# An adaptive-norm mixture-of-experts layer: reloading the higher expert's rows in four stages

## The reference

```python
# condition: base projection plus a low-rank adapter chosen per sequence
c = x @ W.T + b + 2 * ((x @ A[slot]) @ B[slot])          # x: 32 sequences x 32 tokens x 512
# router: 16 experts in 4 groups; the two best groups are kept, then the two best experts
scores = softmax(c @ router_w + router_b) + router_bias
idx = top-2 of the kept scores;  gate = the scores at idx  (zero elsewhere)
for e in 16 experts:                                      # scan
    h = silu(c @ w1[e] + b1[e]) * (c @ w2[e] + b2[e])     # 512 -> 128
    y = y + gate[:, e] * (h @ w3[e] + b3[e])              # 128 -> 512
z = silu(c @ sw1 + sb1) * (c @ sw2 + sb2) @ sw3 + sb3     # shared expert, 512 -> 256 -> 512
out = x + y + z
```

## Time and profile before

| | |
|---|---|
| median of 3 runs | 160.32 us (159.95 to 160.36) |
| the profiled execution | 158.57 us |
| its span, first to last instruction | 156.7 us |
| mean granted TensorE clock | 0.994 |
| busy: PE, DVE, ACT, POOL | 92%, 57%, 42%, 34% |
| HBM read, written | 31.98 MB, 8.91 MB |

### The profile page before, as it was taken

The page is one execution under the profiler, slowest core; times in us unless marked ns, Lnnn a source line. Parts: engine busy times, 40 slices in busy tenths (PEclk is TensorE's granted clock), DMA queues, the critical chain, the costliest instruction groups (busy, mean ns, idle before and its releaser), DMA issues.

```text
span 156.7 us, 3059 instructions
## 1 busy us (share of the span) xinstructions
PE 144.9 (92%) x954; PEld 113.9 (73%) x955; DVE 89.3 (57%) x225; ACT 65.6 (42%) x111; POOL 53.1 (34%) x69
## 2 busy tenths in 40 slices
PE   3999999999989999999999999999897989599990
PEld 3877666877757788888988878887685867188750
DVE  2781484288777679978517434452222240479992
ACT  3542341641722351155876575494554463300000
POOL 7740220000000020536425676667274736340000
PEclk9999999999999999999999999999999999999997
DMA  4989998999985799916541648868685399836993
GB/s 163 355 262 309 409 328 311 345 400 413 418 287 228 228 372 384 391 38 189 145 129 76 193 125 268 287 201 242 226 217 188 105 311 409 319 138 196 375 353 151
DMA packets 16671, 41.09 MB, mean 262 GB/s; under 512 B 2352, under 2 KB 2352, under 8 KB 16528
## 3 DMA queue, kind: packets, MB, share of 16 engines
q1 hardware_dynamic: 11392, 23.33, 42.1%
q0 software_dynamic: 3776, 12.59, 24.9%
q10 hardware_dynamic: 1488, 4.98, 8.3%
HBM read 31.98 MB, written 8.91 MB: 261 GB/s over the span
## 4 chain that ended last, share of the span: by engine, by line
PE 74%; DVE 12%; ACT 4%; issue 4%; another core or an unknown queue 2%; POOL 1%; DVEq 1%; ACTq 1%; POOLq 0%
PE bank L986 27%; PE bank L1166 18%; PE bank L1177 9%; PE bank L1151 5%; DVE x_sb L937 3%; DVE x_sb L950 3%; PE bank L1049 3%; PE bank L1081 2%; PE bank L1029 2%; DVE x_sb L945 2%; PE bank L1039 1%; PE bank L1006 1%; PE bank L1060 1%; PE bank L1141 1%
## 5 line engine op out<-in xcount | busy, mean ns | idle before, releaser
L1166 PE MATMUL bank<-xgT_sb,w_now 128*128 128x128 f32 x288 | 35.2, 275 | 0.0
L1166 PEld LDWEIGHTS bank<-xgT_sb,w_now 128*128 128x128 f32 x288 | 33.6, 192 | 0.6 <-issue 0.5
L875 DVE SCALAR_TENSOR_TENSOR hT_sb<-bank,b_sb,glT_sb 128x128 f32<-128x128 f32 x18 | 6.3, 350 | 38.3 <-ACT glT_sb L614 17.7
L467 POOL DMA_INDIRECT y_rows<-y_ring,slot_row x18 | 19.4, 1079 | 20.5 <-DVE y_ring L883 18.2
L461 POOL DMA_INDIRECT xg_sb<-xt_rows,slot_tok x22 | 21.2, 965 | 13.2 <-issue 5.2
L1177 PE MATMUL bank<-w_sb,hT_sb 128*128 x36 | 18.9, 607 | 4.1 <-DVE hT_sb L875 4.1
L609 ACT COPY w_now<-w_sb 128x1024 f32 x18 | 18.7, 1046 | 3.5 <-issue 2.1
L603 ACT COPY xgT_sb<-bank 128x512 f32<-128x512 f32 x18 | 10.5, 584 | 16.7 <-PE bank L1151 10.6
L1151 PEld LDWEIGHTS bank<-ident,xg_sb 128*128 128x128 f32 x72 | 8.9, 141 | 8.0 <-issue 7.9
L986 PE MATMUL bank<-condW_h,xT_h 128*128 128x512 f32 x32 | 14.4, 449 | 0.0
L986 PE MATMUL bank<-xtT_h,sw_h 128*128 128x512 f32 x32 | 13.2, 412 | 0.0
(11 more groups left out here) (166 smaller groups left out, 240.7 us busy)
## 6 DMA issues: line engine op xcount, KB each, us to landing
w_sb<-in_w SPq DMA_DIRECT2D x8, 1024.0 KB, 10.3
w_sb<-in_w ACTq DMA_DIRECT2D x2, 2048.0 KB, 16.5
xt_rows<-xt_ring SPq DMA_DIRECT2D x8, 256.0 KB, 5.5
x_sb<-in_x SPq DMA_DIRECT2D x8, 256.0 KB
low_sb<-y_rows SPq DMA_DIRECT2D x4, 512.0 KB
high_sb<-y_rows SPq DMA_DIRECT2D x4, 512.0 KB, 5.9
out<-x_sb SPq DMA_DIRECT2D x8, 256.0 KB, 3.2
xT_raw<-in_xT SPq DMA_DIRECT2D x3, 512.0 KB, 8.5
```

Source lines behind the costliest of these rows:

```text
L467: pool.indirect_dma_start(y_rows, bass.IndirectOffsetOnAxis(ap=slot_row[:, b:b + 1], axis=0), y_place(b), None).then_inc(y_scattered[b % Y ...
L875: dve.scalar_tensor_tensor(out=hT_sb[:, s % 2, :], in0=up_bank(s)[:, 0:P], scalar=b12_sb[:, bass.ds(2 * e + 1, 1)], in1=glT_sb[:, s % 2, : ...
L1166: mm = pe.matmul(half[:, 0:P], w12_now[:, s % 2, (2 * k + m) * INTER:(2 * k + m + 1) * INTER], xgT_sb[:, s % 2, k, :], start=(k == 0), sto ...
```

## The change

The one wait for all blocks before the high reload becomes four, one for each pair of tiles. For stages 0 to 2, VectorE works out from `rank` the slot by which every used expert has passed the tokens of that pair of tiles and the earlier ones; stage 3 needs all blocks. With these inputs the stages need 12, 14, 16 and 18 blocks; the low reload needs 10 as before. SP reads 4 low counts and 16 stage counts (20 in place of 8) before the low reload. The high rows are reloaded to a place behind the low rows in `low_sb`, with an address from a register, and `high_sb` is gone. VectorE's tail takes the tiles one by one: low, high, shared; TensorE's wait for banks 5 and 6 is now for the first finished tile.

```diff
@@ names and tiles
-STORED_AT, LOW_STORED_AT = BPAD + 4, BPAD + 4 + Y_RING
+STORED_AT = BPAD + 4
+LOW_STORED_AT = STORED_AT + TILES // 2 * Y_RING
+STAGES = TILES // 2 + 1
-        low_sb = at(0, "low_sb", [P, UPPER_W12 + TILES * DIM])
-        high_sb = at(16, "high_sb", [P, TILES, DIM])
-        diag = at(48, "diag", [P, len(LOW_ON_PE), P])
+        low_sb = at(0, "low_sb", [P, UPPER_W12 + 2 * TILES * DIM])
+        diag = at(104, "diag", [P, len(LOW_ON_PE), P])
-        rows_stored = sem("rows_stored")
+        rows_stored = [sem(f"rows_stored{n}") for n in range(TILES // 2)]
@@ SP
             low_counts = stored(sp, LOW_STORED_AT, LOW_BLOCKS)
-            counts = stored(sp, STORED_AT, FULL)
+            counts = [stored(sp, STORED_AT + n * Y_RING, LOW_BLOCKS) for n in range(TILES // 2)]
@@
-            for s in range(Y_RING):
-                sp.wait_ge(y_scattered[s], counts[s])
-                sp.sem_inc(rows_stored, 1)
-            sp.wait_ge(rows_stored, Y_RING)
             for n in range(TILES // 2):
-                sp.dma_start(high_sb[:, 2 * n:2 * n + 2], by_tile[1][:, 2 * n:2 * n + 2]).then_inc(high_in[n], 16)
+                for s in range(Y_RING):
+                    sp.wait_ge(y_scattered[s], counts[n][s])
+                    sp.sem_inc(rows_stored[n], 1)
+                sp.wait_ge(rows_stored[n], Y_RING)
+                sp.dma_start(low_tiles(first, TILES + 2 * n, 2).rearrange("p (i d) -> p i d", i=2),
+                             by_tile[1][:, 2 * n:2 * n + 2]).then_inc(high_in[n], 16)
@@ VectorE, before the loop
-            then(dve.tensor_scalar(nused_f[:], ends[0:1, E - 1:E], 1.0 / P, None, ALU.mult))
-            then(dve.tensor_scalar(low_base[:], padded[0:1, :], 0, None, ALU.is_gt))
-            then(dve.tensor_tensor(low_base[:], low_base[:], base[0:1, :], ALU.mult))
-            then(dve.tensor_reduce(low_slots[:], low_base[:], AX.X, ALU.max))
+            LAST, LOW = TILES // 2 - 1, TILES // 2
+            then(dve.tensor_scalar(used[:], padded[0:1, :], 0, None, ALU.is_gt))
+            then(dve.tensor_tensor(low_base[:], used[:], base[0:1, :], ALU.mult))
+            then(dve.tensor_tensor(need_e[:], rank[0:1, 2:TILES:2, :], used[:].unsqueeze(1).to_broadcast([1, LAST, E]), ALU.mult))
+            then(dve.tensor_reduce(need[:, LOW:], low_base[:], AX.X, ALU.max))
+            then(dve.tensor_reduce(need[:, 0:LAST], need_e[:], AX.X, ALU.max))
+            then(dve.tensor_copy(need[:, LAST:LOW], ends[0:1, E - 1:E]))
+            then(dve.tensor_scalar(need_i[:], need[:], float(P - 1), None, ALU.add))
+            then(dve.tensor_scalar(need_i[:], need_i[:], P.bit_length() - 1, None, ALU.arith_shift_right))
@@
-            then(dve.tensor_scalar(low_f[:], low_slots[:], 1.0 / P, None, ALU.mult))
-            then(dve.tensor_scalar(stored_i[:, 0], slots_back[:], nused_f[:, 0:1], None, ALU.add))
-            then(dve.tensor_scalar(stored_i[:, 1], slots_back[:], low_f[:, 0:1], None, ALU.add))
+            then(dve.tensor_copy(need[:], need_i[:]))
+            then(dve.tensor_tensor(stored_i[:], need[:].unsqueeze(2).to_broadcast([1, STAGES, Y_RING]),
+                                   slots_back[:].unsqueeze(1).to_broadcast([1, STAGES, Y_RING]), ALU.add))
@@ VectorE's tail: the order of the passes
-            low 0, shared 0, low 1, low 2, shared 1, low 3, shared 2, low 4, shared 3, high 0, high 1,
-            shared 4, high 2, high 3, shared 5, high 4, high 5, high 6, shared 6, high 7, shared 7
+            low 0, high 0, shared 0, low 1, high 1, shared 1, low 2, high 2, shared 2, low 3, high 3, shared 3,
+            low 4, high 4, shared 4, high 5, shared 5, high 6, shared 6, high 7, shared 7
-            (shared adds count acc_shared and wait for it, the last pass of a tile counts acc_done)
+            (every low and high pass waits for itself, every shared add counts acc_done and waits for nothing)
@@ TensorE
                 if shared_bank(i) in (bank[5], bank[6]):
-                    pe.wait_ge(acc_shared, 1)
+                    pe.wait_ge(acc_done, 1)
```

More of the change, by code:

```diff
@@ L189, in program @@
         ngroups = sb("ngroups", [1, 1], I32)
-        nused_f = sb("nused_f", [1, 1])
-        low_f = sb("low_f", [1, 1])
+        used = sb("used", [1, E])
         slots_back = sb("slots_back", [1, Y_RING])
-        stored_i = sb("stored_i", [1, 2, Y_RING], I32)
-        eid = sb("eid", [1, BPAD + 4 + 2 * Y_RING], I32)
+        stored_i = sb("stored_i", [1, STAGES, Y_RING], I32)
+        need_e = sb("need_e", [1, TILES // 2 - 1, E])
+        need = sb("need", [1, STAGES])
+        need_i = sb("need_i", [1, STAGES], I32)
+        eid = sb("eid", [1, BPAD + 4 + STAGES * Y_RING], I32)
         low_base = sb("low_base", [1, E])
-        low_slots = sb("low_slots", [1, 1])
         upper_empty = sb("upper_empty", [1, 1])
-        rows_stored = sem("rows_stored")
+        rows_stored = [sem(f"rows_stored{n}") for n in range(TILES // 2)]
         rank = lgs
@@ L247, in program @@
         y_scattered = [sem(f"y_scattered{s}") for s in range(Y_RING)]
-        shared_done, acc_shared = sem("shared_done"), sem("acc_shared")
+        shared_done = sem("shared_done")
         diag_ready = sem("diag_ready")
@@ L857, in _ @@
             then(dve.tensor_scalar(slots_back[:], cols[0:1, 0:Y_RING], -1.0, float(Y_RING - 1), ALU.mult, ALU.add))
-            then(dve.tensor_scalar(nused_f[:], ends[0:1, E - 1:E], 1.0 / P, None, ALU.mult))
-            then(dve.tensor_scalar(low_base[:], padded[0:1, :], 0, None, ALU.is_gt))
-            then(dve.tensor_tensor(low_base[:], low_base[:], base[0:1, :], ALU.mult))
-            then(dve.tensor_reduce(low_slots[:], low_base[:], AX.X, ALU.max))
+            LAST, LOW = TILES // 2 - 1, TILES // 2
[7 more added lines that the diff above has]
+            then(dve.tensor_scalar(need_i[:], need_i[:], P.bit_length() - 1, None, ALU.arith_shift_right))
             then(dve.tensor_tensor(upper_empty[:], ends[0:1, E - 1:E], ends[0:1, E // 2 - 1:E // 2], ALU.is_equal))
             then(dve.tensor_scalar(eid[0:1, LOW_AT:LOW_AT + 1], upper_empty[:], float(UPPER_W12), None, ALU.mult))
-            then(dve.tensor_scalar(low_f[:], low_slots[:], 1.0 / P, None, ALU.mult))
-            then(dve.tensor_scalar(stored_i[:, 0], slots_back[:], nused_f[:, 0:1], None, ALU.add))
-            then(dve.tensor_scalar(stored_i[:, 1], slots_back[:], low_f[:, 0:1], None, ALU.add))
-            dve.tensor_scalar(eid[0:1, STORED_AT:STORED_AT + 2 * Y_RING], stored_i[:].rearrange("p a s -> p (a s)"),
+            then(dve.tensor_copy(need[:], need_i[:]))
+            then(dve.tensor_tensor(stored_i[:], need[:].unsqueeze(2).to_broadcast([1, STAGES, Y_RING]),
+                                   slots_back[:].unsqueeze(1).to_broadcast([1, STAGES, Y_RING]), ALU.add))
+            dve.tensor_scalar(eid[0:1, STORED_AT:STORED_AT + STAGES * Y_RING], stored_i[:].rearrange("p a s -> p (a s)"),
                               2, 4, ALU.arith_shift_right, ALU.logical_shift_left).then_inc(low_known, 1)
@@ L933, in _, with add_shared @@
             dve.wait_ge(x_in, 16 * TILES)
-            def add_shared(i, last=False):
+            def add_shared(i):
                 dve.wait_ge(shared_done, i + 1)
[L937 to L942, removed]
+                dve.tensor_tensor(x_sb[:, i, :], x_sb[:, i, :], shared_bank(i)[:], ALU.add).then_inc(acc_done, 1)
             def add_low(i):
@@ L946, in add_low, with add_high @@
                                               in1=x_sb[:, i, :], op0=ALU.mult, op1=ALU.add))
-            def add_high(i, last=True):
+            def add_high(i):
                 dve.wait_ge(high_in[i // 2], 16)
[L950 to L955, removed]
+                then(dve.scalar_tensor_tensor(out=x_sb[:, i, :], in0=low_tiles(first, TILES + i), scalar=val[:, 1, i:i + 1],
+                                               in1=x_sb[:, i, :], op0=ALU.mult, op1=ALU.add))
             dve.wait_ge(low_in, 16 * TILES // 2)
             add_low(0)
+            add_high(0)
             add_shared(0)
             add_low(1)
+            add_high(1)
+            add_shared(1)
             add_low(2)
-            add_shared(1)
+            add_high(2)
+            add_shared(2)
             add_low(3)
-            add_shared(2)
+            add_high(3)
+            add_shared(3)
             add_low(4)
-            add_shared(3)
-            add_high(0)
-            add_high(1)
+            add_high(4)
             add_shared(4)
-            add_high(2)
-            add_high(3)
+            add_high(5)
             add_shared(5)
[L973 to L978, removed]
+            add_high(6)
+            add_shared(6)
+            add_high(7)
+            add_shared(7)
         @block.tensor
```

## The result

The changed kernel takes 166.13 us (median of 4 runs, 165.32 to 166.79), the kernel before 160.18 us beside it. The ratio is 1.0484, 95% interval 1.0423 to 1.0546. The profiled execution took 165.77 us, span 163.8 against 156.7, mean granted TensorE clock 0.977. Ratios leave out executions that take over 1.5% more than the fastest of the same kernel.

A forecast was written before the change was run, and what follows sets the result against it. TensorE, busy 92%, was taken to bound the expert loop, with VectorE's tail ending the chain. Late low rows and the first high stage, less the reorder, summed to +2.3 us: 160.9 profiled, 162.6 median, range 159.7 to 164.9.

The forecast's parts named there:

- The index arithmetic: VectorE's small operations before the fourth hidden unit go from 11 to 14, +0.56 us, covered by ScalarE's work: 0.
- The loop: The 18 expert blocks on TensorE gain nothing: 0, bounds -0.5 and +0.5; its end moving over 0.5 us would be wrong.
- SP's loads of counts: Twelve more register loads on SP ahead of the low reload, 0.60 us each, delay its first DMA 7.2 us to 130.5.
- When the low rows land: Low reload beside the last scatters: 2.10 and 0.78 MB at 0.39 MB/us from 132.7, so in place at 140.1.
- rival 3: Worse DMA contention at the reloads: low rows at 142.4, the end 4.8 us later, 165.1 us; chance 0.18.
- High rows, stage 0: First high stage, right behind the low DMAs, lands 1.3 us later at 141.4; VectorE needs it for its second pass.
- Stages 1 to 3: The later high-row reloads land before VectorE needs them and cost 0.
- VectorE's tail: The same 21 passes reordered, 14.9 us from the first high pass; reorder worth -0.3, ending at 156.3, +2.3 us.
- TensorE's wait for a bank: In the tail, it ends with the first tile finished, about 142.9, before the bank is needed at 147.4: 0.
- rival 2: The change pays: the tail's wait for the last high rows goes, -1.0 and -0.3 us, 159.0 us; chance 0.09.
- rival 1: SP's loads cost less, low rows land by 137.9, a delay under about 3.9 us: 160.0 us; chance 0.13.
- The 1.75 us: Timed median 160.32 us above the profiled 158.57; slack for the low rows only if it lies in the last blocks.

The follow-up runs named there:

- e4: The kernel before with its low address and eight counts read by SP before the loads of x; 159.29 us, ratio 1.0034 to the kernel before.
- e3: The kernel before with 12 more register loads, unused, ahead of the low reload; 166.37 us, ratio 1.0455 to the kernel before.
- e1: The changed kernel with each stage's four counts read just before that stage's wait; 157.25 us, ratio 0.987 to the kernel before.
- e9: The kernel of e1 again, on one chip with e10, e11 and e12; 160.46 us, ratio 0.998 to the kernel before.
- e5: The kernel of e1 with the old order of VectorE's passes; 154.18 us, ratio 0.9989 to the kernel before.
- e10: The kernel of e5 again, on the same chip as e9; 159.96 us, ratio 0.994 to the kernel before.
- e2: The changed kernel with the address and all 20 counts read before the loads of x; 158.68 us, ratio 0.984 to the kernel before, resting on two executions.
- e11: The changed kernel itself again, on the same chip as e9; 168.27 us, ratio 1.046 to the kernel before.
- e6: The kernel before with only VectorE's new order of passes, high rows still reloaded in one go; 159.20 us, ratio 1.032 to the kernel before.
- e8: The kernel before with 8 more register loads ahead of the low reload; ratio 1.0366 to the kernel before.
- e12: e9 with low counts read early, tile 0's low pass before the last two blocks, tile 5's low rows moved to VectorE; 161.75 us, ratio 1.007 to the kernel before.

## Why the prediction was wrong

The direction, the mechanism and the place were right: SP's twelve loads hold back the low reload, and VectorE waits for it before its first low pass. What failed is the size of one moment, when the low rows are in place. I had put it at 140.1, and the first low pass began at 145.24, 5.1 us later: 2.9 us of that are the time until SP issues the first low DMA, 2.2 us the time from there until the rows can be used. So the profiled execution took 7.2 us more in place of 2.3, and the median is 166.13 us in place of 162.6, above the range's 164.9. By its own steps:

- *The index arithmetic, 0.* Right: it took 0.57 us more (74.27 to 76.90; before 73.97 to 76.03), as forecast, and the loop's first matmul still begins at 77.15 (76.83 before).
- *The loop, 0.* The last `copy_y` came 1.2 us earlier, beyond the 0.5 that I had named as a sign of being wrong. It doesn't explain the loss, which goes the other way, and no run shows that the change did it: in e4, with the loop of the kernel before, the last `copy_y` came at 135.80, 1.5 us earlier.
- *SP's loads of counts: failed in size.* I put +7.2 us on the first low DMA (0.60 a load), that is 130.5; it was +10.1, 133.4. (14.5 - 5.1)/12 = 0.78 for each added load, and the waits and the first issue took 2.2 in place of 1.8. The loads of the earlier trace rows had a mean spacing of 0.66; I leaned towards the last three and took 0.60. The worst case of 7.9 was also too low: among the twenty loads are single instructions of up to 0.68 us, where the longest of the eight before took 0.37. By the spacing from load to load the trace is near the floor that I had cited; the TENSOR_LOAD row alone, median 0.26 us, is below it, so "agrees" was said of the three instructions together.
- *When the low rows land: failed in size.* I gave 9.6 us from first issue to landing (130.5 to 140.1), by a rate on the bytes. It took 11.8 to the first low pass, and 12.3 in e3. The rows of before held it: first issue at 123.3, last packets near 135.9, 12.6 us. My sum had the 2.2 us to the first packets. It had neither the slow packets behind them (0.10 MB from 134 to 136), nor the 0.84 MB of high rows that moved before the low rows were in place, nor the last few packets. At my rate the 0.84 MB would be 2.2 us, the size of the miss; but e3 took 12.3 without them, so no single one of the three is shown as the cause. With 12.6 and my own 130.5 the sum would have given 143.1.
- *Contention (rival 3): not needed for the loss.* The time fell 1 us above where that rival had put it, 165.1 against 166.1, but the stages that it blames are absent from e3, which loses as much. It is luck that the numbers are close: the low rows came 2.8 us after even that rival's 142.4. How much the scatters beside the reload cost, with or without stages, no run separates.
- *High rows, stage 0.* Right: 1.36 us behind the low rows (146.60 - 145.24; 1.3 forecast), a wait of 0.61. Stages 1 to 3 cost nothing. A slip without effect: in the old order the first high row is the tenth pass, not the eleventh.
- *VectorE's tail.* Right: tile by tile 2.28 us (forecast 2.31), 14.75 from high 0 to the end (146.60 to 161.35; forecast 14.9). TensorE's wait for a bank, forecast at 0, was 1.4 us (before its products of tile 6) and was hidden behind VectorE.
- *Rivals 1 and 2.* Their condition, low rows in time, is not met by the changed kernel. It is met in e1: there the rest of the change is no slower, and beside one chip's kernel it is 1.3% faster, near rival 2's 159.0 of 160.3. On another it gains nothing that can be told (e9). The limit of rival 1 was also summed wrongly: high 0 at 138.8 in place of 141.4 leaves 7.2 - 2.6 = 4.6 us for the loads, 0.38 each, not 3.9 and 0.33.
- *The 1.75 us* between the profiled execution and the median: I put the difference on the median and took them as no slack. The medians moved by 5.95 us, the profiled executions by 7.2. The 1.25 us between the two are what most of that slack would give, but no trace of such an execution shows it. So the median hides a part of the miss, 3.5 us against 4.9 in the profiled execution.

What stays open: how much of e1's 1.3% is the end of the wait for high rows, how much differs from chip to chip, what the drop of the clock takes from it, and what stretches SP's run of loads. Of the changed kernel, reading each stage's counts where they are used is the part whose worth is shown. The stages then cost nothing and gain 0.1 to 1.3% by the four ratios (e1, e5, e9, e10); between the two orders of passes e9 and e10 do not decide (0.998 and 0.994, with intervals that overlap).

## What to carry to other kernels

A register load on a DMA-issuing engine is work in that engine's queue: put each one directly ahead of the wait that needs it, or into a stretch in which the engine waits anyway, never all of them ahead of the first transfer. Price a moved transfer by the issue-to-use time that the same transfer has in the trace, not by its bytes over a rate, and take the slack against the loop's end from more than one execution. A gap of an engine in the timeline is room for work only if its sequencer is waiting in it and not branching or loading registers.

## What the runs showed of the hardware

- A load of one value from SBUF into SP's register, with its register arithmetic and range check, took 0.56 to 0.59 us from load to load early in the expert loop (e4: 8 from 77.4 to 81.3; e2: 20 from 78.8 to 90.0) and 0.74 in the changed kernel (20 from 116.7 to 130.8), with single instructions of up to 0.68 us. The DMA share was 0.42 and 0.50 in e2's and the changed kernel's stretches, so traffic alone is not shown as the cause. The Trainium skill, DMA: Bandwidth & Descriptors, section Latency and other measured facts, has a floor of about 600 ns for a `tensor_load`. The early spacings lie near it and the later ones above it; the TENSOR_LOAD instruction alone had a median of 0.26 us.
- 2.1 MB in four DMAs took 11.8 to 13.6 us from first issue to first use, with high stages in flight (11.8, and 12.0 in e11) or without (12.3 in e3; 13.4 to 13.6 in e6 to e8, on another chip). In the changed kernel, from 134 to 136, the DMA engines were 72% busy and moved 87 GB/s:

```profile
134.00:136.00 2.00, 1.09 (x3) 0.41 (x4) 0.95 (x2) 0.00 (x0) 0.36 (x1) 1.00 0.72 87
```

- TensorE's granted clock fell to 0.50 (1.2 GHz) for about 3 us around the end of the loop in e1, e9 and e12, and not in the kernel before, the changed kernel or e10. In e9 it made the last block's two products take 2.07 us in place of 1.12. TensorE's idle gaps just before were 1.22 and 0.95 us in e9 and 1.07 and 0.94 in the kernel before, whose clock stayed at 1.00. What brings the drop was not tested.
